# Routing chunk 0 of a mixture-of-experts layer ahead of the other chunks' norms, with its sigmoid from exponentials

## The reference

```python
x = x + 0.5 * _L1_ffn_ref(_layernorm(x, axis=-1), ...)

scores = jax.nn.sigmoid(xt.astype(jnp.float32) @ gate_w.T)      # 16 experts
_, idx = lax.top_k(scores + gate_b, 4)
w = jnp.take_along_axis(scores, idx, axis=-1)
w = w / jnp.sum(w, axis=-1, keepdims=True) * 2.5
comb = zeros((T, 16)).at[arange(T)[:, None], idx].add(w)
for each expert e:
    h = silu_and_mul(xt @ w13[e].T)
    y = y + comb[:, e, None] * (h @ w2[e].T)
y = y + silu_and_mul(xt @ w13_s.T) @ w2_s.T                     # shared expert
```

## Time and profile before

| what | us |
|---|---|
| median of 3 runs | 2006.55 (2005.25 to 2006.87) |
| the profiled execution, its own time | 2007.37 |
| its span, first to last instruction | 2006.1 |
| PE busy in the span | 1848.8 (92%) |
| DVE, POOL, ACT busy | 1382.3, 1191.8, 1123.3 |
| mean granted TensorE clock | 0.975 of full speed |

### The profile page before, as it was taken

One profiled execution on the slowest core, in us unless ns is written; L12 is line 12 of the kernel. 1 busy time (PEld: TensorE's weight loads), 2 busy tenths in 40 slices (PEclk: granted clock), 3 DMA queues, 4 the chain that ended last, 5 costly groups with the idle time before them and its releaser, 6 DMA issues. The chain is left out here.

```text
span 2006.1 us, 21942 instructions
## 1 busy us (share of the span) xinstructions
PE 1848.8 (92%) x7360; PEld 1305.5 (65%) x7360; DVE 1382.3 (69%) x2205; ACT 1123.3 (56%) x1587; POOL 1191.8 (59%) x676
## 2 busy tenths in 40 slices
PE   7997999888997967999999999999999999998688
PEld 5873444336875735777777777777777777775366
DVE  5617899976427745677776777777777777774576
ACT  5327777635335455666566666665666556643544
POOL 5541867863535552575666666666667666668444
PEclk9998999999998989999999999999999999999799
DMA  2000000000010033313131322222231313100100
GB/s 94 1 0 0 0 0 0 1 0 0 1 47 1 1 74 82 67 44 73 45 72 45 72 45 54 62 56 61 44 73 40 77 39 71 44 11 12 47 6 17
DMA packets 45683, 74.27 MB, mean 37 GB/s; under 512 B 26561, under 2 KB 28225, under 8 KB 45313
## 3 DMA queue, kind: packets, MB, share of 16 engines
q1 hardware_dynamic: 45104, 72.26, 15.6%
q10 hardware_dynamic: 432, 0.59, 0.1%
q0 software_dynamic: 32, 0.00, 0.0%
HBM read 20.66 MB, written 1.18 MB: 11 GB/s over the span
## 5 line engine op out<-in xcount | busy, mean ns | idle before, releaser
L2234 POOL TENSOR_TENSOR at_e_lo<-at_e,at_e_hi 128x1024 fp32r<-128x1024 f32 x256 | 613.7, 2398 | 380.9 <-DVE at_e_hi L2199 377.7
L2016 ACT ACTIVATE at_e<-at_ps 128x1024 f32<-128x1024 f32 x256 | 263.1, 1028 | 284.9 <-PE at_ps L1922 284.8
L2008 ACT ACTIVATE at_ps<-at_ps,at_neg_diag 128x1024 f32<-128x1024 f32 x256 | 278.6, 1088 | 80.3 <-DVE at_neg_diag L2090 80.3
L2097 DVE TENSOR_REDUCE at_row_max<-at_ps 128x1 f32<-128x1024 f32 x256 | 311.3, 1216 | 5.2 <-PE at_ps L1903 5.2
L2199 DVE CAST at_e_hi<-at_e 128x1024 fp32r<-128x1024 f32 x256 | 257.6, 1006 | 36.8 <-ACT at_e L2016 36.7
L2090 DVE CUSTOM_DVE_ANT_0 at_junk_diag<-at_ps,ident 128x128 bf16<-128x128 f32 x256 | 74.2, 290 | 254.4 <-PE at_ps L1875 253.9
L1047 POOL TENSOR_TENSOR mb_work<-mb_work,mb_c 128x1024 f32<-128x1024 f32 x64 | 151.5, 2368 | 98.3 <-DVE mb_work L1016 96.1
L412 POOL TENSOR_TENSOR ffn_lo<-ffn_hid,ffn_hi 128x512 fp32r<-128x512 f32 x96 | 127.2, 1328 | 133.7 <-DVE ffn_hi L329 133.7
L1873 PE MATMUL at_ps<-at_k,at_q 128*128 128x512 f32 x512 | 162.1, 398 | 19.2 <-DMA at_k<-at_qk_lo 13.5
L1935 PE MATMUL at_pv_ps<-at_e_hi,at_v_hi 128*128 128x512 f32 x512 | 176.5, 426 | 0.3 <-ACT at_pv_sb L2042 0.3
L1903 PE MATMUL at_ps<-at_k,at_q 128*128 128x512 f32 x512 | 162.7, 399 | 11.5 <-DVE at_row_max L2097 8.1
(11 more groups left out here) (356 smaller groups left out, 3803.5 us busy)
## 6 DMA issues: line engine op xcount, KB each, us to landing
at_q<-at_qk_hi SPq DMA_DIRECT2D x64, 256.0 KB, 3.4
at_k<-at_qk_hi SPq DMA_DIRECT2D x32, 512.0 KB, 5.9
at_q<-at_qk_lo SPq DMA_DIRECT2D x32, 256.0 KB, 6.5
at_k<-at_qk_lo SPq DMA_DIRECT2D x32, 256.0 KB, 6.3
at_recips<-at_recip_row SPq DMA_DIRECT2D x31, 256.0 KB, 3.5
ffn_h_raw<-in_h SPq DMA_DIRECT2D x2, 1024.0 KB, 7.4
at_head_w_raw<-in_w_qkv SPq DMA_DIRECT2D x32, 64.0 KB, 4.1
x<-in_x SPq DMA_DIRECT2D x4, 256.0 KB, 6.3
```

What stands on the lines that cost most here:

```text
L2008: act.eng.activation(ps[:], ps[:], ACT.Exp, scale=SCALE, bias=m.small["neg_diag"][s][:, blk:blk + 1], accum_out=m.small["sums"][s][:, blk: ...
L2016: act.eng.activation(m.e[e % 2][:], slot("turned_scores", h, blk)[:], ACT.Exp, scale=SCALE).then_inc(sem["at_exp"])
L2097: dve.eng.tensor_reduce(m.small["row_max"][h % SLOTS][:, blk:blk + 1], slot("best", h, blk)[:], AX.X, ALU.max).then_inc(sem["at_best_out"])
L2234: pool.eng.tensor_tensor(m.e_lo[e % 3][:], m.e[e % 2][:], m.e_hi[e % 3][:].bitcast(F32), ALU.subtract).then_inc(sem["at_lo"])
```

## The change

- `MOE_ROUTE_AT` goes from 3 to 4 and `MOE_SCORES_AT` (the scores of chunks 1 to 3, on ACT) from 2 to 3. The new `MOE_LOGITS_AT = 2` puts the logits of chunks 1 to 3 on PE into step 2 of chunk 0.
- PE does variance 0 ahead of mean 3, and turn 0 between experts 0 and 1.
- ACT does norm 0 behind two squares, then the other squares, x of chunk 0 and scores 0, then the first two splits, norms 1 and 2, turn 0, norm 3, silu 0, the other splits, x of chunk 1, silu 1. x of chunks 2 and 3 move into the loop, to steps 1 and 2.
- Scores 0 are an exponential of the negated logits on ACT; DVE adds 1 and takes the reciprocal. Chunks 1 to 3 keep the sigmoid.
- DVE clears `moe_comb` ahead of centre 3, routes chunk 0 ahead of finishes 1 and 2, and does finish 3 behind product 0. The semaphore `moe_start` counts the two added steps too.

```diff
-MOE_SCORES_AT, MOE_ROUTE_AT, MOE_TURN_AT = 2, 3, 6
+MOE_LOGITS_AT, MOE_SCORES_AT, MOE_ROUTE_AT, MOE_TURN_AT = 2, 3, 4, 6
...
+    for ch in range(3):
+        mean(ch)
+    variance(0)
+    mean(3)
+    for ch in range(1, NCH):
+        variance(ch)
...
     logits(0)
     expert_in(0)
+    turn(0)
     expert_in(1)
-    logits(1)
-    logits(2)
-    turn(0)
-    logits(3)
     for g in range(MOE_G):
...
+        if g == MOE_LOGITS_AT:
+            for ch in range(1, NCH):
+                logits(ch)
...
+    square(0)
+    square(1)
+    inverse(0)
+    square(2)
+    square(3)
     round_xn(0)
-    for ch in range(1, NCH):
-        norm_inverse(act, c, n0 + ch, m.banks[4 + ch], m.inv[ch], m.sq[ch])
     act.wait_ge(sem["moe_logits"], NCH * t + 1)
-    act.eng.activation(m.scores_flat[:, 0:CT * EXPERTS], m.logits_ps[0][:, 0:CT * EXPERTS],
-                       ACT.Sigmoid).then_inc(sem["moe_scores"])
+    act.eng.activation(m.scores_flat[:, 0:CT * EXPERTS], m.logits_ps[0][:, 0:CT * EXPERTS], ACT.Exp,
+                       scale=-1.0).then_inc(sem["moe_scores"])
+    split_weights(0)
+    split_weights(1)
+    inverse(1)
+    inverse(2)
+    turned_out(0)
+    inverse(3)
+    silu(0)
     for i in range(2, len(MOE_W)):
         split_weights(i)
-    for g in range(2):
-        silu(g)
-    for ch in range(1, NCH):
-        round_xn(ch)
-    turned_out(0)
+    round_xn(1)
+    silu(1)
     for g in range(MOE_G):
...
+        if 1 <= g < NCH - 1:
+            round_xn(g + 1)
...
+        if ch == 0:
+            steps = sem["moe_start"]
+            dve.eng.tensor_scalar(m.scores_flat[:, cols], m.scores_flat[:, cols], 1.0, None, ALU.add).then_inc(steps)
+            dve.wait_ge(steps, 3 * t + 2)
+            dve.eng.reciprocal(m.scores_flat[:, cols], m.scores_flat[:, cols]).then_inc(steps)
+            dve.wait_ge(steps, 3 * t + 3)
...
-    for ch in range(NCH):
+    for ch in range(3):
         norm_centre(dve, c, n0 + ch, m.banks[ch], c.x[:, COLS[ch]], m.xn[:, COLS[ch]])
     dve.eng.memset(m.comb[:], 0.0).then_inc(sem["moe_start"])
+    norm_centre(dve, c, n0 + 3, m.banks[3], c.x[:, COLS[3]], m.xn[:, COLS[3]])
     finish(0)
...
-    finish(1)
-    finish(2)
     find_top(0)
     weigh(0)
-    finish(3)
+    finish(1)
     rest_of_turned(0)
+    finish(2)
...
+        if g == 0:
+            finish(3)
```

More of the change, by code:

```diff
@@ L1199, in moe_pe, with mean @@
     n0 = 8 + 8 * t
-    for ch in range(NCH):
+    def mean(ch):
         if t:
@@ L1203, in moe_pe, with variance @@
         norm_mean(pe, c, m.banks[ch], c.x[:, COLS[ch]])
-    for ch in range(NCH):
+    def variance(ch):
         norm_variance(pe, c, n0 + ch, m.banks[4 + ch], m.inv[ch])
+    for ch in range(3):
[4 more added lines that the diff above has]
+        variance(ch)
     def logits(ch):
@@ L1322, in turned_out, with square, inverse @@
         act.eng.activation(m.comb_t[:, COLS[ch]], m.banks[ch % 2], ACT.Copy).then_inc(sem["moe_comb_hi"])
+    def square(ch):
+        norm_square(act, c, n0 + ch, m.xn[:, COLS[ch]], m.inv[ch])
+    def inverse(ch):
+        norm_inverse(act, c, n0 + ch, m.banks[4 + ch], m.inv[ch], m.sq[ch])
     load_logs(act)
[L1325 to L1329, removed]
+    square(0)
[3 more added lines that the diff above has]
+    square(3)
     round_xn(0)
-    for ch in range(1, NCH):
-        norm_inverse(act, c, n0 + ch, m.banks[4 + ch], m.inv[ch], m.sq[ch])
     act.wait_ge(sem["moe_logits"], NCH * t + 1)
-    act.eng.activation(m.scores_flat[:, 0:CT * EXPERTS], m.logits_ps[0][:, 0:CT * EXPERTS],
-                       ACT.Sigmoid).then_inc(sem["moe_scores"])
+    act.eng.activation(m.scores_flat[:, 0:CT * EXPERTS], m.logits_ps[0][:, 0:CT * EXPERTS], ACT.Exp,
[7 more added lines that the diff above has]
+    silu(0)
     for i in range(2, len(MOE_W)):
         split_weights(i)
-    for g in range(2):
-        silu(g)
-    for ch in range(1, NCH):
-        round_xn(ch)
-    turned_out(0)
+    round_xn(1)
+    silu(1)
     for g in range(MOE_G):
@@ L1403, in weigh @@
         dve.wait_ge(route, r + 7)
-        dve.wait_ge(sem["moe_start"], t + 1)
+        dve.wait_ge(sem["moe_start"], 3 * t + 1)
         for start in (0, REST):
```

## The result

| | before | after |
|---|---|---|
| median, us | 2005.99 (4 runs, 2005.25 to 2006.87) | 2030.51 (4 runs, 2028.43 to 2034.20) |
| the profiled execution; its span | 2007.37; 2006.1 | 2028.91; 2027.6 |
| PE, DVE, ACT, POOL busy, us | 1848.8, 1382.3, 1123.3, 1191.8 | 1856.7, 1380.0, 1121.4, 1191.7 |
| mean granted TensorE clock | 0.975 | 0.970 |

The change makes the kernel slower: the ratio is 1.0123, 95% interval 1.0108 to 1.0137, or 24.5 us. No engine has more work (PE's 7.9 us more of busy time are the same matmuls at the lower clock), so the time went into waits and into the clock.

A forecast was written before the change was run, and what follows sets the result against it. It took the layer's body to be bound by PE, its start by a chain of small steps through all engines. A layer: 5.8 + 6.0 + 1.5 = 13.3, two 26.6, giving 2033 us (2014 to 2043).

The forecast's parts named there:

- The routing moved by one product: Turns of chunks 1 to 3: PE idles 3.65 us ahead of each; net 1.93 a turn, 5.8 a layer.
- the 0.38 behind it: PE's idle 0.38 us some three us behind the first two turns, to vanish as product 5 precedes the weighing.
- The clock: Behind each late turn's gap PE runs at the low clock: 2.0 us a turn, 6.0 a layer.
- The upper bound: Clock loss a turn at most 3.2 us, from a granted clock of 0.50 for 6.4 us behind a gap of 3.69.
- The start: Start of each mixture layer: turn 0 earlier but spent before PE's long work; +1.5 us, bounds -2 and +3.
- The moved memset: DVE's clearing ahead of centre 3: lies in time its engine waits; uncovered, costs under 1 us.
- The reciprocal: Chunk 0's scores on DVE, over 128x64: between 0.18 and 0.48 us, taken as 0.48.
- (a): Rival: longer turns don't bring the clock down and the start gains 1 us; +9.6, 2016 us; chance 0.13.
- (b): Rival: turn 0's 6.3 us reach out product 0, turns cost no clock; 2006 us; chance 0.05 with (d).
- (c): Rival: as (b), and later routing is hidden because PE no longer reaches the turn first; 1994 us; chance 0.06.
- (d): Rival: everything is hidden and nothing changes; chance 0.05 together with (b).
- (e): Rival: each low stretch lasts as after 3.69 us, start costs its bound; +37, 2043 us; chance 0.06.

The follow-up runs named there:

- before_route4: The kernel before with MOE_ROUTE_AT 4 instead of 3 and nothing else; ratio 1.0081 to the kernel before, +16.0 us.
- after_fill: The changed kernel with 12 matmuls, result overwritten, ahead of each late turn's wait; ratio 1.0064 to the kernel before, +12.7 us.
- after_split3_fin3: The changed kernel's start with later chunks' routing in three pieces behind products 2, 3, 4 and finish 3 ahead of product 0; ratio 0.9944 to the kernel before.
- after_route3: The changed kernel with MOE_ROUTE_AT back at 3, all else as changed; ratio 1.0027 to the kernel before, +5.7 us.
- after_route3_fin3: The changed kernel with MOE_ROUTE_AT 3 and finish 3 ahead of product 0; ratio 0.9997 to the kernel before, -0.3 us.
- before_split3: The kernel before with later chunks' routing in three pieces behind products 2, 3 and 4; ratio 0.9950 to the kernel before, -10.0 us.

## Why the prediction was right

It said 2033 (2014 to 2043), slower with 0.87; measured are 2030.5. Point by point:

- **The routing moved by one product.** The gap was put at 3.65 for all six. It is 3.62 to 3.63 in four of them and 3.34 to 3.36 in the first of each layer. Given back is the 0.38 behind it. Net 1.9 in four turns and 1.2 in the first two, 5.1 a layer instead of 5.8: the working took the second turn for all three. The first had a gap of 1.72 already and did not move by a whole product: with the constant alone its gap is 3.50, and in the changed kernel PE also reaches it 0.5 later. The constant undone and alone confirms the mechanism.
- **The clock.** Right in kind, too large in size: 2.0 a turn forecast. Turn to turn less 23.6 less 1.9 gives 1.0, 1.3, 2.4 and 2.1, behind the last turns 1.5 and -0.3, so 1.35 a turn, 4 a layer instead of 6. Five of six gaps were followed by the low level, the sixth (1994.82, with 0.66 for its turn) not. Of the kernel before the working said too little, if anything: all ten gaps of 2.65 us or more between 187 and 1817 us, those in the start of the layer and in attention too, had a low stretch at them or right behind; but it is no law, as the sixth turn here and one of before_route4 show. The upper bound was misread: the 0.50 behind the gap of 3.69 belongs to a stretch that was low before (0.50 from 1871.60, behind another gap of 3.53), so it isn't what one gap costs. after_fill shows that the term is real.
- **The start.** Turn 0 was forecast 6.3 earlier and came 6.5 earlier (relative to the first mean); expert 0 was to wait 6 us for POOL's splits and waited 6.07; the first out product was to come 0.1 to 1.7 later and came 0.7 earlier. The term was +1.5 and measured +0.5 and +0.2. Spread 1 came 26.0 us after the first mean, where 26.3 was forecast; what was too large is the logits, 24 passes in 2.75 us instead of 3.6 to 5.0. The moved memset takes 1.76 us and not under 1, without harm here. The reciprocal was 0.55, above my upper bound of 0.48 from 5 ns an element: a straight line through 4 and 8 elements doesn't hold at 64.
- **What the sum left out.** 5.1 + 3.8 + 0.5 = 9.4 and 5.1 + 4.3 + 0.2 = 9.6 are the layers, 19 where I said 26.6. Attention's 4.3 wasn't in it. So the number came out near for a reason that is partly luck: the terms were too large by 8 us, and one was missing with 4.3. (The part before the first layer was 1.7 shorter; the profiled executions differ by 21.5 where 26.6 was forecast, the medians by 24.5.)
- **The rivals.** (a), no clock, falls with after_fill and the windows; (b) and (c), the start paying in full, fall with the first out product, only 0.7 earlier, and with after_split3_fin3; (c) and (d), which hide the later turn, fall with the gaps. (e), every low stretch as long as the longest, falls with the first layer's turns, behind which the clock was low for 3.4 us and then back at 0.92 to 1.00; of the first two turns of layer 2 it is nearly true (losses of 2.4 and 2.1 us).

**What stays open: attention.** Its code and work are the same in all these kernels, but it took 1156.9 to 1163.8 us in the profiled executions. The windows of its first 80 us, in before, after_route3 and after_route3_fin3:

```profile
716.70:796.70 80.00, 51.66 (x174) 33.74 (x175) 39.43 (x99) 45.93 (x76) 27.16 (x33) 0.87 0.44 98
```

```profile
715.80:795.80 80.00, 54.32 (x154) 33.97 (x154) 36.02 (x92) 43.26 (x71) 27.14 (x33) 0.75 0.44 98
```

```profile
716.40:796.40 80.00, 51.53 (x173) 33.66 (x174) 39.33 (x99) 45.86 (x76) 27.17 (x33) 0.87 0.44 98
```

The clock is 0.87, 0.75 and 0.87, and attention takes 1158.7, 1163.8 and 1157.1; in the changed kernel it is 0.82 and 1163.0. It begins with small groups of matmuls and waits, so small shifts may decide whether they run at 1.2 or 2.4 GHz; no run tests this. And the order isn't strict: before_split3 has 0.75 too and 1159.9. Whether the change shifts attention's start to a bad moment each time, or this is chance from one execution to the next, one profile of each kernel can't tell. Two numbers speak for chance: the runs of after_route3 spread from 2006.4 to 2013.2, and its profiled execution, with the longest attention, is the slowest of them, 4.0 above their median. One speaks against it: the changed kernel's profiled execution, with 4.3 us more in attention, is 1.6 below its median. This bears on the 5.7 us left in after_route3, on the 6.0 that after_route3_fin3 took back, and on the part of after_fill's gain that lies outside the layers: none of these is explained by the layers alone.

## What to carry to other kernels

When a change has a headline (route chunk 0 earlier) and a constant beside it, price the constant first: one that acts in every chunk outweighs a start that is paid once. Work that one engine does between two steps of another must fit into the slack of a step; if it doesn't, moving it only chooses who waits. Here pieces of 1.0 to 1.6 us instead of 2.7 took the wait away, in part because they no longer met POOL's steps. And a step that comes 6 us earlier is worth what the last of its companions allows: ask for each engine what it now does later.

## What the runs showed of the hardware

- Behind five of six idle gaps of 3.3 to 3.6 us PE's matmuls of 512 columns start 0.43 us apart instead of 0.23; filling 2.9 us of the gap with matmuls whose result is thrown away kept the granted clock at 1.00 and shortened the stretches from turn to turn by 1.3 to 2.7 us. TensorE: Matmul & The Clock Gate (HAM oscillation) of the Trainium skill warns of waits that make each burst start cold; five of the six turns agree and the sixth doesn't.
- An add or a multiply on DVE with both operands in SBUF, or the cast, that starts while POOL subtracts doesn't end before POOL's step does: the same multiply over 128x64 takes 0.22 to 0.23 alone and 1.26 beside it, the same add 0.22 and 2.17. Not every step is held: the MAX8 and FIND_INDEX8 of the search took 0.16 to 0.18 beside POOL too, and the products, which read PSUM, 0.69. The length of a chain on DVE is thus a matter of when it runs: the same routing took 3.6 us in one place and 5.7 in another.
- A reciprocal takes 0.178 us over 128x4, 0.198 over 128x8 and 0.55 over 128x64, an add with an immediate over 128x64 0.19.
